# First cross attention: operand parts through DRAM, values applied in blocks of four slots, and another opening

## The reference, cut to what matters

```
x = x + xattn(layernorm(x), ctx, ctx, Wq, bq, Wk, bk, Wv, bv, Wo, bo)

qh = (q @ Wq + bq) -> (4, 16, 256, 16);  kh, vh = (ctx @ Wk + bk), (ctx @ Wv + bv) -> (4, 16, 4096, 16)
attn = softmax(qh @ kh^T / 4);  out = attn @ vh;  return concat(out) @ Wo + bo
```

## Time and profile before

| | us |
|---|---|
| median of three runs | 1634.58 |
| profiled execution, its own time | 1630.22 |
| its span, first to last instruction | 1628.4 |
| opening, up to the first score matmul | 82.5 |
| the 512 slots | 873.4 |
| the five later blocks | 672.5 |

### The profile page before, as it was taken

The page is one execution under the profiler, slowest core; times in us unless marked ns, Lnnn a source line. Parts: engine busy times, 40 slices in busy tenths (PEclk is TensorE's granted clock), DMA queues, the critical chain, the costliest instruction groups (busy, mean ns, idle before and its releaser), DMA issues.

```text
span 1628.4 us, 29205 instructions
## 1 busy us (share of the span) xinstructions
PE 1527.5 (94%) x11578; PEld 941.6 (58%) x11578; DVE 1189.0 (73%) x2450; ACT 911.1 (56%) x1469; POOL 340.8 (21%) x459
## 2 busy tenths in 40 slices
PE   6899999999999999999999988999799998699998
PEld 4455555555545555546455455676567787378765
DVE  6788887688886788886888836586365557667767
ACT  4366766666666676666666652476364433246531
POOL 2743232132232132421200021121200002200210
PEclk9799999999999999999999999999899999899999
DMA  3845746356553566464365141000201102000000
GB/s 102 107 53 75 94 53 69 40 65 92 71 60 40 59 85 81 63 70 49 40 79 59 21 146 28 1 1 1 71 8 47 51 1 79 0 1 1 1 1 26
DMA packets 59753, 81.23 MB, mean 50 GB/s; under 512 B 10144, under 2 KB 52384, under 8 KB 53664
## 3 DMA queue, kind: packets, MB, share of 16 engines
q1 hardware_dynamic: 59616, 79.35, 33.5%
HBM read 27.94 MB, written 1.05 MB: 18 GB/s over the span
## 4 chain that ended last, share of the span: by engine, by line
PE 80%; DVE 11%; ACT 4%; issue 3%; POOL 1%; DMA 1%; SPq 0%; DVEq 0%; POOLq 0%; ACTq 0%
PE psum L470 15%; PE psum L435 15%; PE psum L451 13%; PE psum L264 4%; PE psum L545 3%; PE psum L496 3%; PE psum L1968 3%; PE psum L1537 3%; PE psum L1519 3%; PE psum L1257 2%; PE psum L273 2%; DVE peaks L580 2%; PE psum L2016 2%; PE psum L1976 2%; PE psum L2026 1%
## 5 line engine op out<-in xcount | busy, mean ns | idle before, releaser
L580 DVE TENSOR_REDUCE peaks<-psum 128x1 f32<-128x512 f32 x1024 | 661.7, 686 | 148.0 <-PE psum L435 143.9
L696 ACT ACTIVATE probs<-psum 128x1024 f32<-128x1024 f32 x512 | 504.3, 1022 | 156.7 <-PE psum L451 153.9
L435 PE MATMUL psum<-keysT,queriesT 96*128 96x512 bf16 x1024 | 354.3, 386 | 3.7 <-DVE peaks L580 2.5
L451 PE MATMUL psum<-queriesT,keysT 98*128 98x256 bf16 x2048 | 307.8, 272 | 0.3
L470 PE MATMUL psum<-probs,values 128*17 128x256 f32 x4096 | 270.8, 382 | 0.4 <-ACT probs L696 0.4
L451 PEld LDWEIGHTS psum<-queriesT,keysT 98*128 98x128 bf16 x2048 | 194.5, 98 | 104.3 <-issue 21.4
L435 PEld LDWEIGHTS psum<-keysT,queriesT 96*128 96x128 bf16 x1024 | 99.6, 97 | 134.7 <-DVE peaks L580 93.3
L470 PEld LDWEIGHTS psum<-probs,values 128*17 128x17 f32 x4096 | 94.1, 96 | 129.9 <-issue 78.7
L773 POOL CAST key_parts<-key_f 128x512 bf16<-128x512 f32 x56 | 34.3, 612 | 503.8 <-ACT key_f L732 503.3
L1564 DVE TENSOR_REDUCE peaks<-row_w 128x1 f32<-128x512 f32 x64 | 43.6, 683 | 58.6 <-ACT row_w L1623 58.5
L732 ACT ACTIVATE key_f<-psum,bk 128x512 f32<-128x512 f32 x60 | 41.2, 687 | 80.0 <-PE psum L496 77.9
(11 more groups left out here) (249 smaller groups left out, 2123.5 us busy)
## 6 DMA issues: line engine op xcount, KB each, us to landing
keysT<-key_parts SPq DMA_DIRECT2D x372, 128.0 KB, 5.0
ctx_nat<-in_ctx_dram SPq DMA_DIRECT2D x32, 256.0 KB, 3.0
ctx_in<-in_ctx_dram SPq DMA_DIRECT2D x24, 256.0 KB, 4.7
keysT<-key_parts SPq DMA_DIRECT2D x24, 64.0 KB, 2.4
ctxT<-in_x_dram SPq DMA_DIRECT2D x2, 512.0 KB, 5.2
x_old<-in_x_dram SPq DMA_DIRECT2D x2, 512.0 KB, 4.3
w<-in_L_ffn_W_dram SPq DMA_DIRECT2D x2, 512.0 KB, 4.4
w<-in_L_ffn_W_dram SPq DMA_DIRECT2D x1, 1024.0 KB, 7.5
```

The costliest lines, as they stand in the source:

```text
L435: e.matmul(ps, self.queriesT[0:ROWS, i % 4, j, t * P:(t + 1) * P], self.keysT[0:ROWS, i % RING, j, c * BANK:(c + 1) * BANK], start=True, s ...
L451: made = e.matmul(k.psum[:, o:o + S], self.keysT[0:AUG, i % RING, j, kt * P:(kt + 1) * P], self.queriesT[0:AUG, i % 4, j, :], start=True, ...
L580: e.tensor_reduce(self.peaks[:, i % 2, pair, c:c + 1], k.ps(("max", n)), AX.X, ALU.max).then_inc(*self.peaked.up(n))
L696: e.activation(self.probs[:, t % 4, :], k.psum[:, base:base + 2 * BANK], ACT.Exp).then_inc(*self.exped.up(t))
```

## The change

- **Parts go through DRAM.** Every key chunk's three parts are written to a DRAM tensor (`write parts`, one transfer of 384 KB; for unit 0 two, the first group's 32 rows apart), and a group's head rows are read back by six transfers of 256 KB (`read keys`) in the place of 12 of 128 KB. Group 0 is read in five pieces of one or two chunks (`read piece`, 6 transfers each). `key_parts` shrinks to four chunks.
- **Queries** are projected already transposed, with the scale folded into Wq, their parts are written to DRAM (`write queries`), and six transfers per unit bring the rows (`read rows`). `lay rows` and `turn queries` are gone from GpSimd, TensorE and VectorE. Only batch 0 is done in the opening; batches 1 to 3 are normalized, turned and projected in slots 0 to 20.
- **Values** are applied once in four slots (t = 1, 5, 9, ...) in a block of 32 instructions; the ring of probabilities grows from 4 to 6 slots. The values of a batch are made into the other one of two sets, one job in six slots.
- **The opening** begins at slot -60. Unit 0's chunks are split on VectorE and ScalarE together (0, 1, 2, 4, 6) or on GpSimd (3, 5, 7). Group 0's maxima go chunk by chunk. Unit 1's chunks stand at slots -16 to 19. The rows of ones come by transfer and not by GpSimd.
- `LEAD` is 19; `turn shift` is copied by ScalarE; `normalize` stands one slot later.

The core of the diff:

```diff
-LEAD = 18
+LEAD = 19
-FIRST = -101
+FIRST = -60
+RINGP = 6
+    ON_VECTOR = (0, 1, 2, 4, 6)
+    PIECES = ((0, 1), (1, 1), (2, 2), (4, 2), (6, 2))
...
+        for c in range(CH):
+            at(FIRST + 2 * c, "turn ctx", 0, c)
+            at(FIRST + 2 * c + 3, "fill keys", 0, c)
+            at(FIRST + 2 * c + 5, "split rest", c)
+            at(FIRST + 2 * c + 6, "write parts", 0, c)
+            at(-16 + 5 * c, "fill keys", 1, c)
+            at(-14 + 5 * c, "write parts", 1, c)
+        for piece, (c, n) in enumerate(self.PIECES):
+            at(FIRST + 2 * (c + n - 1) + 8, "read piece", piece)
...
+        for b in range(1, B):
+            at(6 * b - 6, "norm x", b)
+            at(6 * b - 3, "turn x", b)
+            at(6 * b, "make queries", b)
+            at(6 * b + 2, "write queries", b)
...
+                at(slot + 2, "fill keys", u, c)
+                at(slot + 6, "write parts", u, c)
+        for u in range(B * KD):
+            at(UNIT * u - 50 if u else FIRST + 12, "read rows", u)
         for i in range(GROUPS):
-            at(SLOTS * i - (32 if i else 38), "load keys", i, 0 if i else CH // 2, CH)
-            at(SLOTS * i - 24, "turn queries", i)
+            if i:
+                at(max(SLOTS * i - 38, -20), "read keys", i)
             at(SLOTS * i - 2, "turn shift", i)
             if i < GROUPS - 1:
-                at(SLOTS * i + SLOTS + 3, "normalize", i)
+                at(SLOTS * i + SLOTS + 4, "normalize", i)
+        for p in range(SLOTS):
+            at(-18 + p, "make values", 0, p)
+            for b in range(1, B):
+                at(SLOTS * NG * b - 97 + 6 * p, "make values", b, p)
...
-            if t % 2 and 3 <= t <= TOTAL + 1:
-                i, p0 = divmod(t - 3, SLOTS)
+            if t % 4 == 1 and 5 <= t <= TOTAL + 1:
+                i, p0 = divmod(t - 5, SLOTS)
...
+                elif job == "write parts":
+                    u, c = a
+                    self.wait_split(w, u, c)
+                    own = slice(c * BANK, (c + 1) * BANK)
+                    to = self.key_dram[u, :, :, own].rearrange("i p n -> p i n")
+                    if u == 0:
+                        e.dma_start(to[0:GROUP_ROWS, :, :], self.key_parts[0:GROUP_ROWS, c % 4, :, :]).then_inc(
+                            *self.first_out[c % 2].up(c))
+                        e.dma_start(to[GROUP_ROWS:P, :, :], self.key_parts[GROUP_ROWS:P, c % 4, :, :]).then_inc(
+                            *self.parts_out[c % 4].up((u, c)))
+                    else:
+                        e.dma_start(to, self.key_parts[:, c % 4, :, :]).then_inc(*self.parts_out[c % 4].up((u, c)))
...
+                elif job == "read keys":
+                    i, = a
+                    u, g = divmod(i, UNIT_GROUPS)
+                    for c in range(CH - 4, CH):
+                        self.wait_written(w, u, c)
+                    if i >= RING:
+                        w.wait_ge(self.scored, SLOTS * (i - RING + 1) - 1)
+                    self.read_keys(e, i, slice(0, LC), self.keys_here[i % RING], i)
...
+    def read_keys(self, e, i, keys, landed, key):
+        u, g = divmod(i, UNIT_GROUPS)
+        rows = slice(g * GH * DH, (g + 1) * GH * DH)
+        for block, part in enumerate(BLOCKS[1]):
+            e.dma_start(self.keysT[block * DH:(block + 1) * DH, i % RING, :, keys],
+                        self.key_dram[u, part, rows, keys].rearrange("(j d) n -> d j n", d=DH)).then_inc(*landed.up(key))
```

More of the change, by code:

```diff
@@ L55, in constants @@
     minus_half, half = np.full((P, NT), -0.5, np.float32), np.full((P, NT), 0.5, np.float32)
[L56 removed]
+    ones = np.full((P, 96), 0x3F803F80, np.uint32).view(np.float32)
+    groups = ([("ident", ident), ("gather", gather), ("minus_half", minus_half), ("half", half), ("ones", ones)],
               [("head_block", head_block), ("head_col", head_col), ("cos", by_tile(cos)), ("sin", by_tile(sin)),
@@ L358, in __init__ @@
         self.due = self.plan()
+        self.chunks = list(self.pool_chunks())
+        self.turns = {chunk: n for n, chunk in enumerate(self.chunks)}
     def plan(self):
@@ L368, in plan @@
+        at(FIRST + 6, "turn x", 0)
+        at(FIRST + 8, "make queries", 0)
+        at(FIRST + 10, "split queries", 0)
+        at(FIRST + 11, "write queries", 0)
+        for b in range(1, B):
[3 more added lines that the diff above has]
+            at(6 * b + 2, "write queries", b)
+        for u in range(2, B * KD):
             b, m = divmod(u, KD)
             for c in range(CH):
-                slot = UNIT * u + FIRST + 8 * c
+                slot = UNIT * u - 101 + 8 * c
@@ L371, in plan @@
                 if m == 0:
-                    if b:
-                        at(slot - 8, "load ctx", b, c)
+                    at(slot - 8, "load ctx", b, c)
                     at(slot, "turn ctx", b, c)
[L375 to L378, removed]
-        for slot, job, t in ((12, "turn norm", 0), (13, "make queries", 0), (20, "turn norm", 4), (28, "make queries", 2),
-                             (36, "make queries", 4), (44, "make queries", 6)):
-            at(FIRST + slot, job, t)
@@ L465, in tensor @@
                 w.wait_ge(self.cleared, 0)
-                for p in (p0, p0 + 1):
+                for p in range(p0, p0 + 4):
                     for e2 in range(2):
@@ L755, in scalar, with pool_chunks @@
+                    e.activation(self.values[:, b % 2, 2 * p:2 * p + 2, :, 0:DH],
                                  k.ps(("v", b, p)).rearrange("p (k h d) -> p k h d", k=2, h=H), ACT.Copy).then_inc(
                         *self.v_kept.up((b, p)))
+    def pool_chunks(self):
+        for t in range(FIRST, TOTAL):
+            for job, *a in self.due.get(t, ()):
+                if job == "fill keys" and not (a[0] == 0 and a[1] in self.ON_VECTOR):
+                    yield tuple(a)
+                elif job == "make queries" and a[0]:
+                    yield "q", a[0]
```

511 lines of the change are left out of this document (261 added, 250 removed).

## The result

The changed kernel takes **1794.03 us** in the median (1791.37 to 1797.02, four runs); the kernel before 1634.14 (1631.77 to 1635.28, four runs). The ratio is 1.098, with a 95% interval of 1.096 to 1.100. I had forecast 1624 in a range of 1582 to 1645. The profiled execution has a span of 1795.2 us.

A forecast was written before the change was run, and what follows sets the result against it. TensorE was taken to set the slots' pace by a small lead over VectorE, while SBUF copies and VectorE maxima end the opening. Opening -15 and slots +5 take the median 1634.58 down by 10, to 1624 us; range 1582 to 1645.

The forecast's parts named there:

- rival C: Slots: group key reads come late once six take over 19.8 us; at 20.8 us the kernel takes 1653 us; chance 0.15.
- The opening, -15: Before the slots: 55 us to group 1's read, 9.5 reading, 3 maxima; first scores at 67.5 us against 82.5.
- my slow bound: Opening: landings paid in full, 13 us of reading and 0.75 us an issue give first scores at 78 us (-4).
- A plain period, 5.84 us: Four plain slots: three maxima banks make TensorE wait for VectorE; 5.84 us, where two old periods cost 5.66.
- rival B: Plain slots: the maxima banks don't bind, a period is 5.46 us and the kernel 1584 us; chance 0.15.
- The slots without the stalls, +5: All slots after the opening: groups -4, values 2, moved queries 5, extra chunk and end block 2, together +5 us.
- queries +5: Early slots: three batches' queries moved in, 13 us of work on two engines, mostly overlapping, 5 on the path.
- unit 1 some +1: Early slots: one more chunk of unit 1, priced together with the longer end block at 2 us.
- groups and values -2: Slots: groups of four periods change by -4 us, values jobs of batches 1 to 3 cost 2 us more.
- end some +1: Last slots: a values block twice as long, priced together with one more unit 1 chunk at 2 us.
- A: Main case: faster opening, long blocks bound by maxima banks; 1624 us, own range 1612 to 1632, chance 0.55.
- D: Opening: many small transfers issued at 1 us rather than 0.63, first scores at 80 us; 1636 us, chance 0.15.

The follow-up runs named there:

- Experiment 1: Changed kernel with key reads from group 3 on back at 32 slots ahead: 1644.99 us; or instead with context loads two slots earlier: 1646.38 us.
- experiment 2: Kernel before the change, with only the key loads from group 3 on listed 38 slots ahead instead of 32: 1804.24 us, ratio 1.105.
- experiment 5: Reads at 32 slots, queries of batches 1 to 3 spread mostly ahead of the slots: 1605.6 us (two-slot blocks), 1638.42 (four); queries behind unit 1, two-slot blocks: 1611.66.
- experiment 3: Changed kernel with key reads back at 32 slots and values applied every two slots instead of four: 1610.25 us, ratio 0.986.

## Why the prediction was wrong

**The step that failed** is the pricing of the reads that were moved six slots up, in rival C. I asked of them only whether they are done in time ("needed 13 slots later", "from the point where the six reads take over 19.8 us"). They are: no maxima wait for them to speak of. What I didn't ask is who stands behind them while they wait. The prediction names no context load at all, and its sum has no term for one, though behind twelve of the 29 reads one stands the next slot in an in-order queue, and the read stays there until five slots past the load's place. The price is 149 us: 111.6 of waiting in twelve places, and by difference 37, or 3.1 for each, behind them, where the clock is at half (40.1 us more of TensorE's busy time say the same). Experiment 1 undoes it in two ways, and experiment 2 gets it from the old kernel by this one number.

**The opening, -15**: right in its number, by luck. First scores are at 66.7 us for 67.5, but the terms missed by some 8 and 7 us in opposite directions. In the profile after, the read of group 1's keys (it has 53 transfers ahead of it, from 13.93 us on) is the first row; the second has the times from issue to landing of its six transfers, the third the first maxima that use it:

```profile
47.04 2.91 SPq L940 DMA_DIRECT2D keysT<-key_parts  x6
...
DMA to landing us min/median/max: 4.6/8.9/12.6
...
62.24 0.59 PE L467 MATMUL psum<-keysT,queriesT 96*128 96x512 bf16 x2
```

The queue is there at 47.0 us and not at 55: an issue takes some 0.5 us rather than 0.63, and the landings held it up for 5.5 us in all, for 7. The read then takes 15.1 us (to 62.1, the last of its landings) and not 9.5, more than the 13 of my slow bound, and from the first maxima of group 1 to the first scores it is 4.5 us for 3. The sum also has no term for TensorE, which waits for the query rows until 34.66 us and is then busy almost without a gap:

```profile
34.70:66.70 32.00, 30.70 (x114) 17.79 (x115) 25.01 (x41) 12.21 (x20) 11.24 (x13) 0.90 0.90 178
```

So a faster read alone would hardly have brought the first scores forward, and it fits that in experiment 5 the queries moved there lengthened the opening by 7.8 us. The fixed cost of about 2 us that the prediction quotes from the Trainium skill (DMA: Bandwidth & Descriptors, Anatomy of one DMA) is given there for transfers that GpSimd issues; these are SyncE's, and no term of the sum hung on it.

**A plain period, 5.84 us**: right, 5.85, and its cause too. With half reductions it falls to 5.47, where I had 5.46 for TensorE alone. So rival B's condition ("the banks don't bind") doesn't hold, and its price is right: of the 48.9 us measured, 9.6 come with any block, which leaves 39.3 for my 40. What I didn't see is that two-slot blocks in the changed kernel are 35 us better. I held 5.84 against 5.66 and let the group come out even, because the shift no longer stalls TensorE. With two-slot blocks that gain isn't given back (23.9 us a group for 24.5 before).

**The slots without the stalls, +5**: mis-sized. With the reads put back they are 902.0 us (67.6 to 969.6) for 873.4, which is +28.6 and not +5:

| stretch of the slots | before | reads put back | of this forecast |
|---|---|---|---|
| first score to slot 32 | 52.4 | 70.2 (+17.8) | queries +5, unit 1 some +1 |
| slot 32 to slot 496 | 802.3 | 807.1 (+4.8) | groups and values -2 |
| slot 496 to the last output | 18.7 | 24.7 (+6.0) | end some +1 |

In the first line the queries are 12.6 us and not 5: "13 us of work on two engines of which most overlaps" was the wrong thought, since TensorE's own share overlaps with nothing while TensorE sets the pace, and it waits for VectorE's share as well. The other 5.2 (57.6 for 52.4 without the queries) I can't split up; the four-slot blocks are 1.3 of them, as 56.3 for 57.6 shows.

In the second line it is the groups with key work. Eight groups in the middle, a whole batch's work and one change of batch, in the kernel before and in that of experiment 1:

```profile
317.58:544.60 227.02, 222.78 (x2017) 120.09 (x2016) 181.76 (x322) 151.50 (x178) 64.10 (x89) 1.00 0.54 66
```

```profile
397.51:626.45 228.94, 223.44 (x1986) 121.13 (x1985) 168.91 (x306) 154.31 (x186) 56.52 (x65) 1.00 0.60 96
```

By my figures the second would be 4 x 26.9 + 4 x 26.1 + 13.1 + 0.8 = 225.9 us. It is 3.0 more, 0.4 for each group. TensorE is idle for 5.5 us of it, where the kernel before has 4.2; that is 1.3 us more, and what the rest is wasn't tried.

The third line is the end, which the prediction had put at some +1 for a block twice as long. In the last 16 slots, the kernel before and that of experiment 1:

```profile
937.20:955.90 18.70, 18.01 (x216) 8.86 (x212) 0.47 (x3) 15.81 (x19) 0.00 (x0) 1.00 0.01 2
```

```profile
944.90:969.60 24.70, 20.04 (x228) 10.46 (x228) 0.47 (x3) 16.36 (x18) 0.00 (x0) 0.93 0.01 1
```

No maxima are left there, and in the kernel before the exponentials set the pace (ScalarE is busy for 15.81 of 18.70 us). With four-slot blocks the two engines wait for each other in turn: ScalarE stands for 1.26 us behind each block until new scores are made, TensorE for 0.68 and 0.30 until ScalarE has emptied a pair of banks. With two-slot blocks (experiment 3) the stretch is 18.9 us.

```profile
960.59 2.85 ACT L717 ACTIVATE probs<-psum 128x1024 f32<-128x1024 f32 x3 [1.26 <-PE psum L483]
961.67 0.61 PE L483 MATMUL psum<-queriesT,keysT 98*128 98x256 bf16 x4 [0.68 <-ACT probs L717]
962.59 0.61 PE L483 MATMUL psum<-queriesT,keysT 98*128 98x256 bf16 x4 [0.30 <-ACT probs L717]
```

**The rivals.** A's mechanism for the blocks held and its time didn't. D is out. C was the right side and the right place in the code, with the wrong mechanism and a fifth of the price (1653 - 1624 = 29 us for 149).

**All in numbers**, medians in us. The last four differ in two things, where the queries stand and how long the blocks are:

| kernel | time | ratio to before |
|---|---|---|
| changed | 1794.0 | 1.098 |
| before, loads six slots earlier | 1804.2 | 1.105 |
| changed, reads at 32 slots | 1645.0 | 1.007 |
| changed, context load two slots earlier | 1646.4 | 1.008 |
| reads at 32, queries spread | 1638.4 | 1.004 |
| reads at 32, two-slot blocks | 1610.3 | 0.986 |
| the same, queries behind unit 1 | 1611.7 | 0.985 |
| the same, queries spread | **1605.6** | **0.982** |

The last one is the change with its reads put back, two-slot blocks and the queries spread; it beats the kernel before by 1.8%.

## What to carry to other kernels

When a transfer that waits is listed earlier on an in-order queue, price not the transfer but the queue: write down everything listed between its new place and the point where its wait ends, and when each of these is needed. That takes one look at the order of the jobs, and here it was worth 149 us, nine times what the opening gave. Second, work that is moved into a stretch that one engine paces is to be priced at that engine's own share in full, and the other engines' shares are hidden only if the pacing engine needn't wait for them: here an estimated 6.9 us of its own became 13. Third, a longer block on the pacing engine needs banks enough that the engine behind it doesn't run dry; alone its saving is an upper bound.

## What I had not expected of the hardware

- After 8.7 us of idleness TensorE ran at half its clock (1.2 of 2.4 GHz), and was at the full one again 5.5 to 10.5 us after its return, though it had been busy without a gap since. By difference (149.0 - 111.6 over twelve stalls) it costs 3.1 us behind each, a third on top of the stall.
- Six transfers of 256 KB are issued in 2.84 us and twelve of 128 KB in 12.78, and yet a 256 KB load issued behind them reaches TensorE at nearly the same time, 15.9 and 17.8 us after the first of them. I read it as the bytes ahead that decide; that was not tried with other sizes, and in the changed kernel a chunk write of 384 KB and the next load are issued right behind it and may have slowed it.
